# A recurrence on one core: one scan and one subtraction for both halves of the state, instead of two scans and a subtraction

## The chip, the cores and the metric

The kernel runs on one core of a Trainium2 chip. Its engines are TensorE (PE in the profile; its weight loads stand apart as PEld), VectorE (DVE), ScalarE (ACT), GpSimd (POOL) and SyncE (SP, which issues DMAs). They run side by side and wait for each other by semaphores. The metric is the device time of one execution in microseconds (us).

## The reference

Four graph layers follow each other on 1250 nodes with 512 features, each with a residual and a layer norm. The change touches only the recurrence in the first layer:

```
def gru(x_seq, W_ih, W_hh, b_ih, b_hh):
    pre_i = x_seq @ W_ih.T + b_ih            # 1250 x 1536
    def step(h, pi):
        ph = h @ W_hh.T + b_hh
        r = sigmoid(pi[:H] + ph[:H])
        z = sigmoid(pi[H:2*H] + ph[H:2*H])
        n = tanh(pi[2*H:] + r * ph[2*H:])
        h_new = (1.0 - z) * n + z * h
        return (h_new, h_new)
    _, ys = scan(step, zeros(H), pre_i)      # H = 512, 1250 steps, one after the other
```

## The kernel before

**Stages.** The edges are counted into dense adjacency matrices, two graph convolutions follow, then the input side of the recurrence (`pre_i`, kept in `big`), then the recurrence itself, then the other three layers. Each stage waits for the one before it, so a stage's time adds to the whole.

**The state.** The 512 elements of the state lie on 128 partitions as four blocks of 128. Two blocks form a half: c (of outputs) or kc (of inputs) is 0 or 1. The products are made in f16, with weights and state each split into a high and a low part. `h16` holds the state's parts. The weights' parts are in `whh16`: gates r and z (g = 0, 1) in memory that the profile names r, gate n (g = 2) in memory that it names hn. DVE holds the state scaled by HS = 4096.

**A product.** `gru_gate(u, c, kc, g)` issues, for gate g, the products of state half kc into output half c: two output blocks j by two input blocks k by two parts of the weights. One product is a 128x128 weight load and a matmul whose moving data is the state's one or two columns, repeated 16 times (COPIES). The low weights (part 1) meet the high state alone: 16 columns. The high weights (part 0) meet both: 32 columns. The results go to PSUM bank 4c + g, with the second output block at column offset 3 for gates r and z and at offset 4 for gate n. All low-weight products of a gate come before its high-weight products.

**Order on TensorE in a step.** Half 0 of the state into gates r, z, n of output half 0 (24 products), into r of half 1 (8) and half of n of half 1 (4); then half 1 of the state into r, z, n of half 0 (24), into r of half 1 (8); the other half of n (4), half 1 into n (8); last the z gate of half 1 (8 + 8). That is 96. Waits stand ahead of the first products that use the high part of a state half (`gru_state` 2t + 1), again ahead of the first that use its low part (2t + 2), and ahead of gates whose PSUM columns ScalarE fills with `pre_i` and bias (`gru_put0`, `gru_put1`).

**The rest of a step, for each half.** DVE adds the columns of r and of z with a scan of 6 elements (`scan_rz`, line 997); ScalarE takes the sigmoids (lines 719 and 724); DVE scans n's 8 columns with r as factor (`scan_n`, line 1003); ScalarE takes the tanh (line 728). Then DVE's `update` (line 1011) scans 8 elements, four per block, to the new state; `high_part` (line 1014) runs the same scan again with f16 output; `low_part` (line 1020) subtracts the high part from the f32 value. POOL (lines 328 and 329) prepares the next update's addends and keeps the state in `r1`. ScalarE's `put` (line 706) writes the next step's inputs into PSUM: three calls after the r sigmoid of half 1, two at the end. Each engine runs its instructions in the written order.

Of the kernel before, what the change touches and what calls it, by code (L numbers as in the profile page):

```python
# [25 lines left out]
ACT = mybir.ActivationFunctionType  # L26
# [8 lines left out]
P = 128  # L35
# [9 lines left out]
HS = 4096.0  # L45
XS = 2.0 ** 10
# [8 lines left out]
def layout(nc, io):  # L55

    ctx = ExitStack()
    with ctx:
# [99 lines left out]
        h16 = sb("h16", [P, 2, 2, 16], F16)  # L158
# [6 lines left out]
        upd_mul = sb("upd_mul", [P, 2, 8])  # L165
        upd_add = sb("upd_add", [P, 2, 8])
        upd = sb("upd", [P, 2, 2, 8])
# [35 lines left out]
        def _(sp):  # L203
# [44 lines left out]
            for c in range(2):  # L248
                sp.wait_ge(s(f"gru_put{c}"), (N + 1) * (1, 3)[c])
# [35 lines left out]
        def _(pool):  # L285
# [35 lines left out]
            with pool.Fori(0, N // 2) as i:  # L321
                for u in range(2):
                    t = 2 * i + u
                    for c in range(2):
                        pool.wait_ge(s(f"gru_state{c}"), 2 * t + 3)
                        pool.wait_ge(s(f"gru_upd{c}"), t + 1)
                        new, start = (a.rearrange("p (j a) -> p j a", a=4) for a in (upd[:, 1 - u, c], upd_add[:, c]))
                        pool.tensor_tensor(start[:, :, 1:3], new[:, :, 2:3].broadcast_to([P, 2, 2]), signs[:].rearrange("p (j a) -> p j a", a=2), ALU.mult).then_inc(s(f"gru_fresh{c}"), 1)  # L328
                        pool.tensor_copy(r1[:, 2 * c:2 * c + 2, bass.ds(t, 1)], upd[:, 1 - u, c, 2:8:4]).then_inc(s(f"gru_kept{c}"), 1)  # L329
# [20 lines left out]
        def _(pe):  # L350
# [141 lines left out]
            def gru_gate(u, c, kc, g, pieces=every, part=None):  # L492

                if part is None:
                    gru_gate(u, c, kc, g, pieces, 1)
                    return gru_gate(u, c, kc, g, pieces, 0)
                for j, k in pieces:
                    at = (4 if g == 2 else 3) * j
                    places = psum[:, 4 * c + g, 0:8 * COPIES].rearrange("p (r a) -> p r a", a=8)[:, :, at:at + 2 - part]
                    state = h16[:, u, kc, 8 * k + 6:8 * k + 8 - part]  # L500
                    m = mm(places, whh16[g][:, part, 2 * kc + k, (2 * c + j) * P:(2 * c + j + 1) * P],  # L501
                           state.unsqueeze(1).broadcast_to([P, COPIES, 2 - part]), start=(kc == 0 and j == 0 and k == 0 and part == 1),
                           stop=(kc == 1 and k == 1 and part == 0), skip_group_check=True)
# [769 lines left out]
```

## Time and profile before

| | |
|---|---|
| median of 3 runs | 5311.0 us (5308.29 to 5320.85) |
| the profiled execution | 5311.0 us, span 5308.3 us |
| the recurrence in the span | about 782 to 4172 us |
| busy over the span | PE 96%, PEld 81%, DVE 56%, ACT 41%, POOL 18% |
| mean granted TensorE clock | 0.961 of full speed |

The page lists groups of instructions by source line. Matmuls are pipelined: the profile shows each from its start to its modelled end, so they overlap, and how densely they are issued is seen in the starts or in the number of them in a stretch, not in the busy time. "Idle before" is an engine's idle time ahead of an instruction, with what ended it.

### The profile page before, as it was taken

What the parts mean: (1) busy time and instruction counts of PE and PEld (TensorE: products, weight loads), DVE (VectorE), ACT (ScalarE), POOL (GpSimd) and SP (SyncE); (2) the same over time, 40 slices, a digit from 0 to 9 for tenths busy, and PEclk for the clock granted to TensorE, in tenths of its full rate; (3) what the DMA queues carried; (4) which work ended last, traced back from release to release, by engine and by line L of the source; (5) the groups of instructions that cost most, each with busy time, mean ns of one, the idle gap of its engine ahead of it and who ended that gap; (6) DMA issues with size and microseconds to landing.
All of it is one profiled execution on the core that took longest, in us unless ns stands there. A gap on an engine that the chain in (4) does not pass through costs nothing.

```text
span 5308.3 us, 338777 instructions
## 1 busy us (share of the span) xinstructions
PE 5099.5 (96%) x128234; PEld 4274.3 (81%) x128235; DVE 2948.9 (56%) x16450; ACT 2160.5 (41%) x15422; POOL 948.7 (18%) x5221
## 2 busy tenths in 40 slices
PE   6669999999999999999999999999999999999989
PEld 4555559999999999999999999999999645555654
DVE  6662336666666666666666666666666444455551
ACT  0110005555555555555555555555555201221110
POOL 1230002222222222222222222222222100000000
PEclk7559999999999999999999999999999999999989
DMA  1002220000000000000000000000000100000011
GB/s 59 0 4 96 79 87 0 0 0 0 0 0 0 0 0 0 0 0 0 0 0 0 0 0 0 0 0 0 0 0 0 54 2 16 35 35 35 19 46 45
DMA packets 28930, 81.07 MB, mean 15 GB/s; under 512 B 1594, under 2 KB 1834, under 8 KB 28858
## 3 DMA queue, kind: packets, MB, share of 16 engines
q1 hardware_dynamic: 28858, 80.03, 4.1%
q8 instruction: 55, 0.90, 0.1%
q14 instruction: 17, 0.14, 0.0%
HBM read 58.08 MB, written 21.95 MB: 15 GB/s over the span
## 4 chain that ended last, share of the span: by engine, by line
PE 92%; DVE 3%; issue 2%; DVEq 2%; ACT 0%; POOL 0%; DMA 0%; SPq 0%; POOLq 0%; ACTq 0%
PE psum L501 64%; PE psum L570 8%; PE psum L376 5%; PE psum L366 4%; PE psum L582 4%; PE psum L483 2%; PE psum L556 2%; PE psum L646 1%; PE psum L423 1%; DVE r L879 1%; DVEq L874 1%; DVE r L878 1%; DVEq L872 1%; DVEq L871 1%; PE psum L433 0%
## 5 line engine op out<-in xcount | busy, mean ns | idle before, releaser
L501 PE MATMUL psum<-h,r 128*128 128x16 f16 (+1 forms) x80000 | 3087.7, 181 | 9.1 <-DVE h L1014 4.4
L501 PEld LDWEIGHTS psum<-h,r 128*128 128x128 f16 x80000 | 2555.9, 96 | 125.6 <-ACT psum L706 5.0
L501 PE MATMUL psum<-h,hn 128*128 128x16 f16 (+1 forms) x40000 | 1798.1, 177 | 0.0
L501 PEld LDWEIGHTS psum<-h,hn 128*128 128x128 f16 x40000 | 1416.7, 96 | 0.0
L997 DVE TENSOR_TENSOR_SCAN sum_rz<-mul_rz,psum 128x6 f32<-128x6 f32 x5000 | 814.6, 163 | 570.1 <-PE psum L501 511.5
L719 ACT ACTIVATE mul_n<-sum_rz 128x2 f32<-128x2 f32 x2500 | 517.7, 207 | 1198.9 <-DVE sum_rz L997 1198.9
L328 POOL TENSOR_TENSOR upd_add<-upd,signs 128x4 f32<-128x4 f32 x2500 | 500.5, 200 | 2731.3 <-DVE h L1014 1566.7
L706 ACT COPY psum<-big 128x2 f32 (+1 forms) x7506 | 931.0, 158 | 0.0
L1011 DVE TENSOR_TENSOR_SCAN upd<-upd_mul,upd_add 128x8 f32<-128x8 f32 x2500 | 437.0, 175 | 528.3 <-ACT upd_mul L724 373.0
L728 ACT ACTIVATE upd_add<-sum_n 128x2 f32<-128x2 f32 x2500 | 516.5, 207 | 271.5 <-DVE sum_n L1003 268.7
L724 ACT ACTIVATE upd_mul<-sum_rz 128x2 f32<-128x2 f32 x2500 | 493.7, 197 | 7.5
L1003 DVE TENSOR_TENSOR_SCAN sum_n<-mul_n,psum 128x8 f32<-128x8 f32 x2500 | 426.9, 171 | 122.2
L329 POOL COPY r<-upd 128x2 f32 x2500 | 470.8, 188 | 0.0
L1020 DVE TENSOR_TENSOR h<-upd,h 128x2 f16<-128x2 f32 x2500 | 421.9, 169 | 85.4
L1014 DVE TENSOR_TENSOR_SCAN h<-upd_mul,upd_add 128x8 f16<-128x8 f32 x2500 | 408.4, 163 | 0.0
L423 PE MATMUL psum<-r 125*128 125x100 bf16 x2580 | 238.3, 270 | 68.6 <-DVE r L879 62.0
L423 PEld LDWEIGHTS psum<-r 125*128 125x128 bf16 x2580 | 191.4, 132 | 109.8 <-DVE r L879 109.1
L376 PE MATMUL psum<-adj,hn 125*128 125x417 f32 (+1 forms) x720 | 252.7, 512 | 2.1 <-ACT hn L671 1.4
L376 PEld LDWEIGHTS psum<-adj,hn 125*128 125x128 f32 x720 | 135.7, 189 | 119.6 <-issue 115.0
L878 DVE TENSOR_SCALAR r<-r,hn 125x1254 bf16<-125x1254 f16 x258 | 151.7, 588 | 138.9 <-issue 101.1
L570 PE MATMUL psum<-adj,r 128*125 128x512 f16 x960 | 220.7, 388 | 8.3 <-DVE r L1199 8.3
L570 PEld LDWEIGHTS psum<-adj,r 128*125 128x125 f16 x960 | 133.5, 139 | 89.5 <-issue 16.2
(231 smaller groups left out, 2791.4 us busy)
## 6 DMA issues: line engine op xcount, KB each, us to landing
ws<-in_Wl SPq DMA_DIRECT2D x9, 1024.0 KB, 5.3
ws<-in_Wr SPq DMA_DIRECT2D x9, 1024.0 KB, 8.4
edge_counts<-adj SPq DMA_DIRECT2D x2, 3051.8 KB
edge_weights<-big SPq DMA_DIRECT2D x1, 6103.5 KB
adj_rows<-big SPq DMA_DIRECT2D x1, 6103.5 KB
adj<-adj_rows SPq DMA_DIRECT2D x1, 6103.5 KB
big<-edge_counts SPq DMA_DIRECT2D x1, 6103.5 KB
adj<-edge_weights SPq DMA_DIRECT2D x1, 6103.5 KB
```

The costliest lines, as they stand in the source:

```text
L328: pool.tensor_tensor(start[:, :, 1:3], new[:, :, 2:3].broadcast_to([P, 2, 2]), signs[:].rearrange("p (j a) -> p j a", a=2), ALU.mult).then ...
L329: pool.tensor_copy(r1[:, 2 * c:2 * c + 2, bass.ds(t, 1)], upd[:, 1 - u, c, 2:8:4]).then_inc(s(f"gru_kept{c}"), 1)
L376: m = mm(o[:, 0:n1 - n0], rows[0:NP, t, f * P:(f + 1) * P], mat[0:NP, t, n0:n1], start=(t == 0), stop=(t == NT - 1))
L423: m = mm(psum[:, 2 * u + t // 5, (t % 5) * 100:(t % 5) * 100 + 100], src_hot[0:EP, h, t * NP:t * NP + P], dst_hot[0:EP, h], start=False, s ...
L501: m = mm(places, whh16[g][:, part, 2 * kc + k, (2 * c + j) * P:(2 * c + j + 1) * P], state.unsqueeze(1).broadcast_to([P, COPIES, 2 - part] ...
L570: m = mm(o, a(pa), b(pb), start=start and i == 0, stop=stop and i == 2)
L706: return nc.scalar.copy(columns, big[:, bass.ds(t * 12 + c * 6 + 2 * g, 2)])
L719: nc.scalar.activation(mul_n[:, c, 3:8:4], sum_rz[:, c, 0, 2:6:3], ACT.Sigmoid).then_inc(s(f"gru_r{c}"), 1)
L724: nc.scalar.activation(upd_mul[:, c, 2:8:4], sum_rz[:, c, 1, 2:6:3], ACT.Sigmoid).then_inc(s(f"gru_z{c}"), 1)
L728: nc.scalar.activation(upd_add[:, c, 0:8:4], sum_n[:, c, 3:8:4], ACT.Tanh).then_inc(s(f"gru_n{c}"), 1)
L997: v.tensor_tensor_scan(sum_rz[:, c, g], mul_rz[:], psum[:, 4 * c + g, 0:6], 0.0, ALU.mult, ALU.add).then_inc(s(f"gru_{'rz'[g]}_sum{c}"), 1)
L1011: v.tensor_tensor_scan(upd[:, 1 - u, c], upd_mul[:, c], upd_add[:, c], 0.0, ALU.mult, ALU.add).then_inc(s(f"gru_upd{c}"), 1)
```

## The change

- The update scan becomes 14 elements, seven per block. After the new state and its multiple by 4096 it adds and takes away ROUND = 1.5 x 2^24, which leaves the value rounded to a coarse grid (the high part), and then a zero. The second scan is gone.
- One subtraction, `new_state`, yields for each block the pair (scaled state less high part, high part less zero), which is (low, high), in f16.
- There is one `gru_state` signal per half and step. TensorE no longer begins on the high part alone.
- Every product moves both columns: the low weights meet the low part too, 32 columns for all 96. The order within a gate goes over the parts innermost.
- ScalarE puts n's inputs of half 1 ahead of the z gate of half 1, and the signals are regrouped: `gru_put1` for r and n together, `gru_putz1` for z.
- POOL waits for the update scan alone. Strides of the update's arrays go from 4 to 7.

```
-            def gru_gate(u, c, kc, g, pieces=every, part=None):
-                if part is None:
-                    gru_gate(u, c, kc, g, pieces, 1)
-                    return gru_gate(u, c, kc, g, pieces, 0)
+            def gru_gate(u, c, kc, g, pieces=every):
                 for j, k in pieces:
                     at = (4 if g == 2 else 3) * j
-                    places = psum[:, 4 * c + g, 0:8 * COPIES].rearrange("p (r a) -> p r a", a=8)[:, :, at:at + 2 - part]
-                    state = h16[:, u, kc, 8 * k + 6:8 * k + 8 - part]
-                    m = mm(places, whh16[g][:, part, 2 * kc + k, (2 * c + j) * P:(2 * c + j + 1) * P],
-                           state.unsqueeze(1).broadcast_to([P, COPIES, 2 - part]), ...)
+                    for part in range(2):
+                        m = mm(psum[:, 4 * c + g, 0:8 * COPIES].rearrange("p (r a) -> p r a", a=8)[:, :, at:at + 2],
+                               whh16[g][:, part, 2 * kc + k, (2 * c + j) * P:(2 * c + j + 1) * P],
+                               h16[:, u, kc, k].unsqueeze(1).broadcast_to([P, COPIES, 2]), ...)
...
-                    pe.wait_ge(s("gru_state0"), 2 * t + 1)
+                    pe.wait_ge(s("gru_state0"), t + 1)
                     pe.wait_ge(s("gru_put0"), t + 1)
-                    gru_gate(u, 0, 0, 0, part=1)
-                    pe.wait_ge(s("gru_state0"), 2 * t + 2)
-                    gru_gate(u, 0, 0, 0, part=0)
-                    for g in (1, 2):
+                    for g in range(3):
                         gru_gate(u, 0, 0, g)
-                    pe.wait_ge(s("gru_put1"), 3 * t + 1)
+                    pe.wait_ge(s("gru_put1"), t + 1)
                     gru_gate(u, 1, 0, 0)
-                    pe.wait_ge(s("gru_put1"), 3 * t + 2)
                     gru_gate(u, 1, 0, 2, every[:2])
-                    pe.wait_ge(s("gru_state1"), 2 * t + 1)
-                    gru_gate(u, 0, 1, 0, part=1)
-                    pe.wait_ge(s("gru_state1"), 2 * t + 2)
-                    gru_gate(u, 0, 1, 0, part=0).then_inc(s("gru_r_mm0"), 1)
+                    pe.wait_ge(s("gru_state1"), t + 1)
+                    gru_gate(u, 0, 1, 0).then_inc(s("gru_r_mm0"), 1)
...
-                    pe.wait_ge(s("gru_put1"), 3 * t + 3)
+                    pe.wait_ge(s("gru_putz1"), t + 1)
...
-                    put(t + 1, 1, 0).then_inc(s("gru_put1"), 1)
+                    put(t + 1, 1, 0)
                     gate_n(1)
+                    put(t + 1, 1, 2).then_inc(s("gru_put1"), 1)
                     gate_z(1)
-                    put(t + 1, 1, 2).then_inc(s("gru_put1"), 1)
-                    put(t + 1, 1, 1).then_inc(s("gru_put1"), 1)
+                    put(t + 1, 1, 1).then_inc(s("gru_putz1"), 1)
...
-            def high_part(u, c):
-                v.tensor_tensor_scan(h16[:, 1 - u, c, 0:16:2], upd_mul[:, c], upd_add[:, c], 0.0, ALU.mult, ALU.add).then_inc(s(f"gru_state{c}"), 1)
-            def low_part(t, u, c):
-                dve.wait_ge(s(f"gru_state{c}"), 2 * t + 3)
+            def new_state(t, u, c):
                 dve.wait_ge(s(f"gru_upd{c}"), t + 1)
-                v.tensor_tensor(h16[:, 1 - u, c, 7:16:8], upd[:, 1 - u, c, 3:8:4], h16[:, 1 - u, c, 6:16:8], ALU.subtract).then_inc(s(f"gru_state{c}"), 1)
+                new = sevens(upd[:, 1 - u, c])
+                v.tensor_tensor(h16[:, 1 - u, c], new[:, :, 3:6:2], new[:, :, 5:7], ALU.subtract).then_inc(s(f"gru_state{c}"), 1)
```

## Rows read from the trace of the kernel before

**Rows 1.** The page: costliest groups and the chain that ended last, by line.
```profile
PE psum L501 64%; PE psum L570 8%; PE psum L376 5%; PE psum L366 4%; PE psum L582 4%; PE psum L483 2%; PE psum L556 2%; PE psum L646 1%; PE psum L423 1%; DVE r L879 1%; DVEq L874 1%; DVE r L878 1%; DVEq L872 1%; DVEq L871 1%; PE psum L433 0%
...
L501 PE MATMUL psum<-h,r 128*128 128x16 f16 (+1 forms) x80000 | 3087.7, 181 | 9.1 <-DVE h L1014 4.4
...
L501 PE MATMUL psum<-h,hn 128*128 128x16 f16 (+1 forms) x40000 | 1798.1, 177 | 0.0
```

**Rows 2.** Windows by stage: length, busy us (instructions) of PE, PEld, DVE, ACT, POOL; clock.
```profile
782.00:4172.00 3390.00, 3383.89 (x120000) 3267.90 (x120000) 2084.09 (x15000) 1911.81 (x15007) 808.51 (x4998) 1.00 0.00 0
```

**Rows 3.** Timeline over one step: start us, us, engine, line (DVE, ACT, POOL).
```profile
3000.24 0.17 DVE L1020 TENSOR_TENSOR h<-upd,h 128x2 f16<-128x2 f32 x1
...
3001.50 0.21 ACT L728 ACTIVATE upd_add<-sum_n 128x2 f32<-128x2 f32 x1
...
3001.74 0.17 DVE L1011 TENSOR_TENSOR_SCAN upd<-upd_mul,upd_add 128x8 f32<-128x8 f32 x1
3001.77 0.35 ACT L706 COPY psum<-big 128x2 f32 x3
3001.83 0.16 DVE L1014 TENSOR_TENSOR_SCAN h<-upd_mul,upd_add 128x8 f16<-128x8 f32 x1
3002.03 0.17 DVE L1020 TENSOR_TENSOR h<-upd,h 128x2 f16<-128x2 f32 x1
3002.13 0.17 DVE L1003 TENSOR_TENSOR_SCAN sum_n<-mul_n,psum 128x8 f32<-128x8 f32 x1
3002.16 0.20 POOL L328 TENSOR_TENSOR upd_add<-upd,signs 128x4 f32<-128x4 f32 x1 [1.55 <-DVE h L1014]
3002.21 0.15 DVE L997 TENSOR_TENSOR_SCAN sum_rz<-mul_rz,psum 128x6 f32<-128x6 f32 x1
...
3002.33 0.21 ACT L728 ACTIVATE upd_add<-sum_n 128x2 f32<-128x2 f32 x1 [0.21 <-DVE sum_n L1003]
3002.44 0.19 ACT L724 ACTIVATE upd_mul<-sum_rz 128x2 f32<-128x2 f32 x1
3002.54 0.24 ACT L706 COPY psum<-big 128x2 f32 x2
...
3002.66 0.17 DVE L1011 TENSOR_TENSOR_SCAN upd<-upd_mul,upd_add 128x8 f32<-128x8 f32 x1 [0.30 <-ACT upd_mul L724]
...
3004.44 0.17 DVE L1011 TENSOR_TENSOR_SCAN upd<-upd_mul,upd_add 128x8 f32<-128x8 f32 x1
```

**Rows 4.** The same timeline, TensorE's matmuls merged by tile.
```profile
3000.41 0.59 PE L501 MATMUL psum<-h,r 128*128 128x16 f16 x16
...
3002.79 0.38 PE L501 MATMUL psum<-h,r 128*128 128x16 f16 x8
...
3003.11 0.58 PE L501 MATMUL psum<-h,r 128*128 128x16 f16 x16
...
3003.53 0.36 PE L501 MATMUL psum<-h,hn 128*128 128x16 f16 x8
...
3003.95 0.46 PE L501 MATMUL psum<-h,hn 128*128 128x16 f16 x12
...
3004.26 1.20 PE L501 MATMUL psum<-h,r 128*128 128x16 f16 x32
```

**Rows 5.** Windows: weight loads (xN), then matmuls (xN) seen in growing stretches.
```profile
3002.03:3002.12 0.09, 0.00 (x0) 1.00 0.00 0
3002.03:3002.13 0.10, 0.01 (x1) 1.00 0.00 0
3002.03:3002.25 0.22, 0.13 (x4) 1.00 0.00 0
3002.03:3002.26 0.23, 0.14 (x5) 1.00 0.00 0
...
3001.90:3001.95 0.05, 0.05 (x9) 1.00 0.00 0
3001.90:3001.96 0.06, 0.06 (x10) 1.00 0.00 0
3001.90:3002.13 0.23, 0.23 (x10) 1.00 0.00 0
3001.90:3002.14 0.24, 0.24 (x11) 1.00 0.00 0
...
3002.15:3002.25 0.10, 0.10 (x4) 1.00 0.00 0
3002.15:3002.26 0.11, 0.11 (x5) 1.00 0.00 0
...
3002.15:3003.71 1.56, 1.56 (x59) 1.00 0.00 0
3002.15:3003.72 1.57, 1.57 (x60) 1.00 0.00 0
```

**Rows 6.** Views by line: durations in ns, min/median/max.
```profile
L997 DVE TENSOR_TENSOR_SCAN sum_rz<-mul_rz,psum x5000: 149/167/168, 784.3 to 4171.3; 128x6 f32<-128x6 f32 x193
...
L1003 DVE TENSOR_TENSOR_SCAN sum_n<-mul_n,psum x2500: 169/171/172, 784.8 to 4171.2; 128x8 f32<-128x8 f32 x193
...
L1011 DVE TENSOR_TENSOR_SCAN upd<-upd_mul,upd_add x2500: 173/175/191, 785.3 to 4171.8; 128x8 f32<-128x8 f32 x193
...
L1020 DVE TENSOR_TENSOR h<-upd,h x2500: 168/168/171, 785.5 to 4172.1; 128x2 f16<-128x2 f32 x193
```

**Rows 7.** Views by line of two kinds of sequencer instruction, same columns.
```profile
L510 PEldq ALU_OP  x1250: 32/34/36, 782.4 to 4168.4; - x179
...
L1002 DVEq EVENT_SEMAPHORE  x2500: 21/21/21, 784.7 to 4171.2; - x193
```

**Rows 8.** Groups by line and shape, 1000 to 4500 us: busy us, mean ns of one.
```profile
L501 PE MATMUL psum<-h,r 128*128 128x32 f16 x37496 | 2339.8, 184 | 0.0
L501 PE MATMUL psum<-h,r 128*128 128x16 f16 x37496 | 2297.0, 178 | 0.0
...
L501 PE MATMUL psum<-h,hn 128*128 128x32 f16 x18752 | 1301.3, 176 | 0.0
L501 PE MATMUL psum<-h,hn 128*128 128x16 f16 x18752 | 1273.5, 178 | 0.0
```

**Rows 9.** View of line 501, 1000 to 4000 us: ns min/median/max.
```profile
L501 PE MATMUL psum<-h,r x70944: 176/177/193, 1000.0 to 3999.8; 128*128 128x16 f16 x100, 128*128 128x32 f16 x100
...
L501 PE MATMUL psum<-h,hn x35481: 176/177/181, 999.8 to 4000.0; 128*128 128x16 f16 x100, 128*128 128x32 f16 x100
```

More of the change, by code:

```diff
@@ L45 @@
 HS = 4096.0
+ROUND = 1.5 * 2.0 ** 24
 XS = 2.0 ** 10
@@ L162, in layout @@
         sum_n = sb("sum_n", [P, 2, 8])
[L165 to L167 removed]
+        upd_mul = sb("upd_mul", [P, 2, 14])
+        upd_add = sb("upd_add", [P, 2, 14])
+        upd = sb("upd", [P, 2, 2, 14])
         signs = sb("signs", [P, 4])
@@ L324, in _ @@
                     for c in range(2):
-                        pool.wait_ge(s(f"gru_state{c}"), 2 * t + 3)
                         pool.wait_ge(s(f"gru_upd{c}"), t + 1)
-                        new, start = (a.rearrange("p (j a) -> p j a", a=4) for a in (upd[:, 1 - u, c], upd_add[:, c]))
+                        new, start = (a.rearrange("p (j a) -> p j a", a=7) for a in (upd[:, 1 - u, c], upd_add[:, c]))
                         pool.tensor_tensor(start[:, :, 1:3], new[:, :, 2:3].broadcast_to([P, 2, 2]), signs[:].rearrange("p (j a) -> p j a", a=2), ALU.mult).then_inc(s(f"gru_fresh{c}"), 1)
-                        pool.tensor_copy(r1[:, 2 * c:2 * c + 2, bass.ds(t, 1)], upd[:, 1 - u, c, 2:8:4]).then_inc(s(f"gru_kept{c}"), 1)
+                        pool.tensor_copy(r1[:, 2 * c:2 * c + 2, bass.ds(t, 1)], upd[:, 1 - u, c, 2:14:7]).then_inc(s(f"gru_kept{c}"), 1)
             def roots(n0, n1):
@@ L490, in _ @@
             every = ((0, 0), (0, 1), (1, 0), (1, 1))
-            def gru_gate(u, c, kc, g, pieces=every, part=None):
-                if part is None:
-                    gru_gate(u, c, kc, g, pieces, 1)
-                    return gru_gate(u, c, kc, g, pieces, 0)
+            def gru_gate(u, c, kc, g, pieces=every):
                 for j, k in pieces:
                     at = (4 if g == 2 else 3) * j
-                    places = psum[:, 4 * c + g, 0:8 * COPIES].rearrange("p (r a) -> p r a", a=8)[:, :, at:at + 2 - part]
-                    state = h16[:, u, kc, 8 * k + 6:8 * k + 8 - part]
-                    m = mm(places, whh16[g][:, part, 2 * kc + k, (2 * c + j) * P:(2 * c + j + 1) * P],
-                           state.unsqueeze(1).broadcast_to([P, COPIES, 2 - part]), start=(kc == 0 and j == 0 and k == 0 and part == 1),
-                           stop=(kc == 1 and k == 1 and part == 0), skip_group_check=True)
+                    for part in range(2):
+                        m = mm(psum[:, 4 * c + g, 0:8 * COPIES].rearrange("p (r a) -> p r a", a=8)[:, :, at:at + 2],
+                               whh16[g][:, part, 2 * kc + k, (2 * c + j) * P:(2 * c + j + 1) * P],
+                               h16[:, u, kc, k].unsqueeze(1).broadcast_to([P, COPIES, 2]), start=(kc == 0 and j == 0 and k == 0 and part == 0),
+                               stop=(kc == 1 and k == 1 and part == 1), skip_group_check=True)
                 return m
@@ L710, in _ @@
             put(0, 0, 2).then_inc(s("gru_put0"), 1)
-            for g in (0, 2, 1):
-                put(0, 1, g).then_inc(s("gru_put1"), 1)
+            put(0, 1, 0)
+            put(0, 1, 2).then_inc(s("gru_put1"), 1)
+            put(0, 1, 1).then_inc(s("gru_putz1"), 1)
             with act.Fori(0, N // 2) as i:
@@ L981, in _ @@
             link(v.memset(upd_mul[:], 1.0))
-            link(v.memset(upd_mul[:, :, 0:8:4], 0.0))
-            link(v.memset(upd_mul[:, :, 3:8:4], HS))
+            link(v.memset(upd_mul[:, :, 0:14:7], 0.0))
+            link(v.memset(upd_mul[:, :, 3:14:7], HS))
+            link(v.memset(upd_mul[:, :, 6:14:7], 0.0))
             link(v.memset(upd_add[:], 0.0))
+            link(v.memset(upd_add[:, :, 4:14:7], ROUND))
+            link(v.memset(upd_add[:, :, 5:14:7], -ROUND))
             link(v.memset(signs[:], 1.0))
@@ L991, in _, with sevens @@
             for c in range(2):
-                dve.sem_inc(s(f"gru_state{c}"), 2)
+                dve.sem_inc(s(f"gru_state{c}"), 1)
                 dve.sem_inc(s(f"gru_fresh{c}"), 1)
+            def sevens(ap):
+                return ap.rearrange("p (j a) -> p j a", a=7)
             def scan_rz(t, c, g):
```

18 lines of the change are left out of this document (9 added, 9 removed).

## The prediction

> **What bounds the kernel now.** I read the page first. The 1250 steps of the recurrence hold 120,000 of the 128,234 matmuls, and line 501 carries 64% of the chain that ended last [rows 1]. The windows by stage put the recurrence at 782 to 4172 us of the span, 3390 of 5308 us, with a granted clock of 1.00 [rows 2]: any change here is a number of nanoseconds per step, times 1250. "PE busy 100%" says nothing by itself, since one matmul is shown for some 177 ns and the next starts after some 26, so a pause shorter than that is invisible in the busy time. So I went to single steps.
>
> One step lasts from one update scan of column half 0 to the next, 3001.74 to 3004.44, 2.70 us [rows 3]. A step has 2 x 2 x 3 x 4 x 2 = 96 products (a weight load and a matmul each). The pieces of the TensorE timeline give their spacing: 16 products on the r tile in 3003.11 to 3003.53 (26.3 ns each), 12 on the hn tile in 3003.95 to 3004.26 (25.8 ns each) [rows 4]. At 26 ns, 96 products need 2.50 us, so 0.2 us per step is a pause. The windows that count products find it: the last of a step starts at 3001.96, the first of the next only at 3002.13; four have started by 3002.25, and only then does the fifth [rows 5]. That is the start of a step: product 1 waits for the high part of the new state (scan of line 1014, 3001.83 to 3002.00), product 5 for the low part (subtraction of line 1020, ends 3002.20) [rows 3].
>
> So the step is a loop of three stretches, and I use it for the sum. From the update scan's start to product 5: 3001.74 to 3002.26, 0.52 us. From product 5 to product 60, the last of the n gate of half 0 (24 + 8 + 4 + 24 = 60 products in issue order): 3002.26 to 3003.72, 1.46 us [rows 5]. From product 60 to the next update scan (matmul latency, scan, tanh): 3003.72 to 3004.44, 0.72 us [rows 3]. Together 2.70 us. TensorE's products 61 to 96 lie beside the third stretch and end before it does; that is the pause.
>
> Half 1 has a chain of its own. Its state is needed at product 37. Its low part ended at 3000.41, so product 41 could start at 3000.47; it started at about 3000.41 + 4 x 0.026 = 3000.51, in its turn [rows 3, 4]. It is near the bound, but it stops nothing: the spacing there stays 26 ns.
>
> **The change part by part.**
>
> *DVE.* The second scan (line 1014) goes. The update scan gets 14 elements instead of 8, and the subtraction that follows yields both f16 parts, 4 elements instead of 2. The 6-element scans take 167 ns and the 8-element ones 171 from PSUM: 2 ns an element [rows 6]; so the 14-element one takes 175 + 6 x 2 = 187 ns. The subtraction takes 168 for 2 elements [rows 6]; I add 2 to 4: 171. A dependent instruction starts some 30 to 40 ns after what it waits for (high part's end 3002.00, subtraction 3002.03; tanh's end 3001.71, update scan 3001.74) [rows 3]; I take 34. So both parts are there at 187 + 34 + 171 = 392 ns after the update scan's start. Before, the high part was there after 0.26 us (3001.74 to 3002.00) and the low part after 0.46. The complete state comes **64 ns sooner**, the high part alone 0.13 us later. If a scan element cost 1 or 4 ns, the 64 would be 70 or 52.
>
> *TensorE's wait.* Product 1 carries two waits, on the state and on the added-in inputs (gru_put0). Before, from the high part's end to its weight load were 3002.00 to 3002.12, some 0.12 us; product 5, with one wait, had its load at 3002.25 to 3002.26 after the low part's end at 3002.20, 0.05 to 0.06 us [rows 3, 5]. gru_put0 was no reason: ScalarE's three copies run from 3001.77 at 0.09 us spacing and the second, which is the one waited for, ends by 3002.03. The difference is a sequencer instruction between the two waits, the register operation of line 510, 34 ns long [rows 7]. In the changed code both waits compare with t + 1, so that operation should fall away, but the first wait still needs a carrier; on DVE a bare wait of this kind takes 21 ns [rows 7]. I take 0.12 - 0.013 = 0.11 us. So product 1's load now comes at 392 + 110 = 502 ns, its matmul 7 ns later: **0.51 us** after the update scan, where product 5 stood at 0.52. The bounds are 0.46 us (one wait's 0.057) and 0.52.
>
> *The early products.* Here is the price. Before, products 1 to 4 (low weights times the high part) were done when the low part came; now product 1 begins where product 5 began. **Four products more stand in the loop: 4 x 25.8 = 103 ns.**
>
> *Width.* The 48 products with the low weights now move 32 columns, not 16, and write both columns of a place. On width alone I add nothing: on the hn tile a 32-column matmul shows 176 ns and a 16-column one 178 [rows 8], and both kinds keep the spacing of 25.8. But on the r tile, where gates r and z are, the 32-column matmuls show 184 on average [rows 8]. Half of them (first output block, offset 0) should be like hn's 176, so the other half, whose pair of columns starts at offset 3, takes 192; the maximum of the r rows is 193, of the hn rows 181 [rows 9]. Offset 3 is odd, the n gate's second block starts at 4. The spacing shows a trace of it: 16 products with 4 such pairs took 0.42 us where 16 at hn's spacing would take 0.413 [rows 4], so 2 to 5 ns for each odd pair; I take 3.5. The change turns two odd pairs per r or z gate into four. The stretch from product 1 to 60 holds five such gates: **10 x 3.5 = 35 ns**. Bounds: 0 (the queue swallows it) and 10 x 16 = 160 ns (each shows its full 192 - 176). I stay near the spacing, as spacing is what the loop adds up.
>
> The Trainium skill bears on this: "PSUM — Partial Sum Buffer", Memory Cachelines, says PSUM has lines of two fp32 values and that every two consecutive elements should lie together for best throughput. A pair at offset 3 lies over two lines, and the trace agrees (192 against 176 ns). By that rule doubling the odd pairs is a real cost and the full 16 ns each, 160 per step, would be added if writing were the limit; by the spacing row it is 35. The rule speaks against the change in either case.
>
> *Reordered work.* ScalarE's copy into the n gate of half 1 is put ahead of the z gate of half 1, so that one semaphore covers r and n. It delays z's sigmoid, and so the second update scan, by one copy's spacing, 0.09 us. Behind it, DVE's queue is shorter by the removed scan (0.09 us) with 12 ns lost to the longer one, and the n scan of half 1, its tanh and the sigmoid come some 0.07 us sooner. Net: the second update scan moves from 0.92 us after the first (3002.66) to 0.94, its state is there at 0.94 + 0.39 = 1.33, usable at 1.39. Product 37 stood 0.98 us behind product 1 (3003.11 less 3002.13, a stop within), and comes now at 0.51 + 0.95 + 0.02 = 1.48 [rows 3 to 5]. No stall: worth nothing, with 0.09 us to spare. If the extra copy cost 0.19 us instead of 0.09, the cover would be gone. gru_put1 now comes after the tanh, near 3002.5 on the old clock, and product 25 needs it at 3002.79 [rows 4]; the queue behind that wait is all the rest of the step, but it is met. POOL starts up to 0.1 us sooner; it is idle 1.5 us before its pair of instructions and nobody waits for it. Its work, and removed sequencer work on all engines, lie off the loop: nothing. Set-up adds three small memsets, under 1 us.
>
> **Sum per step.** Update scan to product 1: 0.51. Product 1 to 60: 1.46 + 0.103 + 0.035 = 1.60. Product 60 to the next update: 0.72. Total 2.83 against 2.70. By differences: -64 (state) + 53 (two waits instead of one: 110 - 57) + 103 + 35 = **+127 ns**. Times 1250: +159 us. The profiled execution took 5311.0 us (span 5308.3 and 2.7 around it), which is also the median of the three, so 5311 + 159 = **5470 us**, 3.0% slower.
>
> **Rivals.**
> 1. *Slower, but less: the odd pairs cost nothing more and the wait is as short as product 5's.* For: the 7 ns of the spacing row are less than the view's rounding of 10. -35 alone gives +92 ns, 5426; with the short wait too (-53) +39 ns, 5360. 15%.
> 2. *Slower, and more: odd pairs in a row cost their shown 16 ns.* Four in sequence leave no room to catch up, which the trace of before, with two, never shows. +125 ns more: 5470 + 156 = 5626; half of it 5548. 15%. The skill's rule above is this rival at its full size.
> 3. *Faster: half 1 sets the step.* If the true setter were the state of half 1 (it ended at 3000.41 with its products right behind), then its chain's gain of 64 - 20 = 44 ns a step would be the result: 5311 - 55 = 5256. It decides if a pause stands before product 37. Against it: the pause of 0.17 us stands before product 1, and none before 37. 4%. From half 0's side a gain is out of reach: product 1 would have to start 0.13 us sooner than computed, at 0.38 us, and the subtraction ends at 0.39.
> 4. *No change.* The spacing of a stream of only 32-column products falls to 25 ns and the odd pairs vanish with the change of shape: 59 x 0.8 + 35 = 82 ns off, +45 ns; with the short wait (-53) it comes to -8 ns, 5301. It needs three lucky terms. 5%.
> 5. *The clock.* The pause grows from 0.17 to some 0.29 us per step. If the chip answered with 1.2 GHz instead of 2.4, all would be far slower. Against it: the granted clock is 1.00 over the recurrence with its pauses of 0.17 us [rows 2], and the columns moved rise by a third (2304 to 3072 a step). 1%.
>
> My forecast holds 60%, its own range 5430 to 5515.
>
> **Numbers.** 0.3% (16 us) is what a measurement of this kernel can tell from no change. Slower: 60 + 15 + 15 + 1 = 91%, less a little for rival 1's lower end: 90%. Same 6%, faster 4%. The range must leave out no more than 2 in 10: from 5370, within rival 1, to 5565, within rival 2.
>
> **What would show it.** The update scan at 185 to 190 ns and no second scan; the subtraction ending 0.39 us after its start; no products for 0.29 us at the start of a step, then no second stop after product 4; 16 products on the r tile in 0.43 to 0.44 us instead of 0.42; 32-column matmuls on r at 184 on average or a little more; a step of 2.83 us. I am wrong if product 1 starts less than 0.1 us after the state, if r products come 25 ns apart (both less), or if they come over 28 apart, or if a stop appears before product 37 (more).

## The result

The changed kernel takes 5340.93 us (median of 5 runs, 5339.82 to 5343.85), the kernel before 5309.69 us in the same comparison. The ratio is 1.0057, with a 95% interval of 1.0044 to 1.0072: slower by 31 us, clear of no change by a small margin. Forecast were 5470 us, with a range from 5370 to 5565. The sign was right and the size wrong by a factor of five, so the time lies below the range. In steps: 2.74 us instead of 2.70, where 2.83 was forecast.

The windows by stage put the excess where it was expected: the recurrence takes 3425 us (779 to 4204) instead of 3390, at a granted clock of 1.00 [rows 2]. The page of the changed kernel shows one new figure next to those of before [rows 1]: TensorE's idle time "before" rises from 9 to 44 us, since the pause at the start of a step (0.225 us from product 96 to product 1, 0.172 before) is now longer than the 193 ns that the step's last matmul is shown for.

```profile
L498 PE MATMUL psum<-h,r 128*128 128x32 f16 x80000 | 3109.0, 184 | 44.3 <-ACT psum L699 4.9
L498 PEld LDWEIGHTS psum<-h,r 128*128 128x128 f16 x80000 | 2539.7, 96 | 192.6 <-DVE h L1017 64.9
L498 PE MATMUL psum<-h,hn 128*128 128x32 f16 x40000 | 1776.1, 177 | 0.0
```

The timeline over one step of the changed kernel answers to [rows 3, 4]. Line 1011 is the update scan, line 1017 the one subtraction.

```profile
3001.40 0.19 DVE L1011 TENSOR_TENSOR_SCAN upd<-upd_mul,upd_add 128x14 f32<-128x14 f32 x1
3001.42 0.35 ACT L699 COPY psum<-big 128x2 f32 x3
3001.62 0.16 DVE L1017 TENSOR_TENSOR h<-upd 128x4 f16<-128x4 f32 x1
...
3002.28 0.35 PE L498 MATMUL psum<-h,hn 128*128 128x32 f16 x8
...
3002.33 0.19 DVE L1011 TENSOR_TENSOR_SCAN upd<-upd_mul,upd_add 128x14 f32<-128x14 f32 x1 [0.32 <-ACT upd_mul L718]
...
3002.80 0.59 PE L498 MATMUL psum<-h,r 128*128 128x32 f16 x16
...
3003.23 0.35 PE L498 MATMUL psum<-h,hn 128*128 128x32 f16 x8
...
3004.14 0.19 DVE L1011 TENSOR_TENSOR_SCAN upd<-upd_mul,upd_add 128x14 f32<-128x14 f32 x1
```

And the windows that count matmuls, as in [rows 5]: in those from 3001.55 the count stays at 10 from 3001.62 to 3001.83 and then product 1 comes; in those from 3001.86, where only product 1 and its followers are in sight, product 60 is the 60th, just before 3003.42.

```profile
3001.55:3001.61 0.06, 0.06 (x9) 1.00 0.00 0
3001.55:3001.62 0.07, 0.07 (x10) 1.00 0.00 0
3001.55:3001.83 0.28, 0.26 (x10) 1.00 0.00 0
3001.55:3001.84 0.29, 0.26 (x11) 1.00 0.00 0
3001.86:3003.40 1.54, 1.54 (x59) 1.00 0.00 0
3001.86:3003.41 1.55, 1.55 (x59) 1.00 0.00 0
3001.86:3003.42 1.56, 1.56 (x60) 1.00 0.00 0
```

So the subtraction ends at 3001.78, and product 1 starts at 3001.84, 0.06 us later. The forecast had 0.117. The loop's three stretches, in us; the measured ones are means over 1000 steps of each trace, from the starts of the same instructions:

| stretch | before | forecast | after |
|---|---|---|---|
| update scan to the full state's end | 0.457 | 0.392 | 0.384 |
| from there to the product that needs it | 0.063 (product 5) | 0.117 (product 1) | 0.057 (product 1) |
| that product to product 60 | 1.461 | 1.598 | 1.573 |
| product 60 to the next update scan | 0.725 | 0.72 | 0.725 |
| a step | 2.706 | 2.83 | 2.739 |

Two terms are off: the wait by 60 ns, the products by 25. The experiments take these, and the terms that came out right, one by one.

### The profile page after: what moved, and what is told of

Its sections match the earlier page's. It is cut to its first block, busy times and chain, and to the rows that moved or that the text cites. A ratio compares the mean times of both kernels' runs of the same rounds, so it can differ in the third digit from the quotient of the medians.

```text
span 5341.3 us, 325031 instructions
## 1 busy us (share of the span) xinstructions
PE 5093.8 (95%) x128234; PEld 4238.2 (79%) x128235; DVE 2851.6 (53%) x13953; ACT 2171.7 (41%) x15422; POOL 956.0 (18%) x5221
## 4 chain that ended last, share of the span: by engine, by line
issue 57%; PE 21%; POOL 13%; POOLq 3%; DVE 3%; DVEq 2%; ACT 0%; DMA 0%; SPq 0%; ACTq 0%
PE psum L563 8%; POOL upd_add L329 7%; POOL r L330 6%; PE psum L575 4%; PE psum L367 3%; POOLq L330 2%; PE psum L549 2%; PE psum L377 2%; PE psum L639 1%; PE psum L424 1%; DVE r L873 1%; DVEq L868 1%; POOLq L323 1%; DVE r L872 1%; DVEq L866 1%
## 5 line engine op out<-in xcount | busy, mean ns | idle before, releaser
L498 PE MATMUL psum<-h,r 128*128 128x32 f16 x80000 | 3109.0, 184 | 44.3 <-ACT psum L699 4.9
L498 PE MATMUL psum<-h,hn 128*128 128x32 f16 x40000 | 1776.1, 177 | 0.0
L498 PEld LDWEIGHTS psum<-h,hn 128*128 128x128 f16 x40000 | 1395.5, 96 | 0.0
L997 DVE TENSOR_TENSOR_SCAN sum_rz<-mul_rz,psum 128x6 f32<-128x6 f32 x5000 | 834.1, 167 | 693.0 <-PE psum L498 630.5
L699 ACT COPY psum<-big 128x2 f32 (+1 forms) x7506 | 1022.8, 158 | 0.0
L1011 DVE TENSOR_TENSOR_SCAN upd<-upd_mul,upd_add 128x14 f32<-128x14 f32 x2500 | 467.8, 187 | 544.7 <-ACT upd_mul L718 395.7
L718 ACT ACTIVATE upd_mul<-sum_rz 128x2 f32<-128x2 f32 x2500 | 508.2, 203 | 14.0 <-DVE sum_rz L997 0.2
L1017 DVE TENSOR_TENSOR h<-upd 128x4 f16<-128x4 f32 x2500 | 409.7, 164 | 86.0
L367 PE MATMUL psum<-ws,r 128*125 128x512 f32 x400 | 179.9, 612 | 7.2 <-ACT r L740 5.9
```

What stands on the lines that cost most here:

```text
L498: m = mm(psum[:, 4 * c + g, 0:8 * COPIES].rearrange("p (r a) -> p r a", a=8)[:, :, at:at + 2], whh16[g][:, part, 2 * kc + k, (2 * c + j) * ...
L699: return nc.scalar.copy(columns, big[:, bass.ds(t * 12 + c * 6 + 2 * g, 2)])
L718: nc.scalar.activation(upd_mul[:, c, 2:14:7], sum_rz[:, c, 1, 2:6:3], ACT.Sigmoid).then_inc(s(f"gru_z{c}"), 1)
L997: v.tensor_tensor_scan(sum_rz[:, c, g], mul_rz[:], psum[:, 4 * c + g, 0:6], 0.0, ALU.mult, ALU.add).then_inc(s(f"gru_{'rz'[g]}_sum{c}"), 1)
L1011: v.tensor_tensor_scan(upd[:, 1 - u, c], upd_mul[:, c], upd_add[:, c], 0.0, ALU.mult, ALU.add).then_inc(s(f"gru_upd{c}"), 1)
```

## The experiments

Times are medians; each ratio is to the kernel before, run on the same chip in turn, with its 95% interval. Steps and spacings given to the nanosecond are means over 1000 steps of the run's trace.

### Are the early products the price? (e3)

```
-                    pe.wait_ge(s("gru_state0"), 2 * t + 1)
                     pe.wait_ge(s("gru_put0"), t + 1)
-                    gru_gate(u, 0, 0, 0, part=1)
                     pe.wait_ge(s("gru_state0"), 2 * t + 2)
-                    gru_gate(u, 0, 0, 0, part=0)
-                    for g in (1, 2):
+                    for g in range(3):
                         gru_gate(u, 0, 0, g)
```

> The kernel before, but the first gate of a step no longer starts on the high part: TensorE waits for gru_put0 and the low part of half 0's state, and then issues all of gate r. Theory (products 1 to 4 done early are worth their issue time in the loop): product 1 starts where product 5 started, 0.52 us after the update scan, the step grows by 4 x 26 = 104 ns to 2.81 us, the time to about 5440. Rival (the restart of TensorE costs something each time it stops, so that one stop instead of two gives part back): 5400 to 5425. Rival (the early products were not in the loop): 5310.

Measured: 5437.41 us, ratio 1.0240 (1.0224 to 1.0257). The step is 2.807 us, 100 ns longer. The timeline shows it plainly (line 1017 is the subtraction here): the low part is ready at 3001.77, and the first weight load of the step, with all 60 products of the loop still to come, starts at 3001.82, after 0.22 us in which no weight load ran.

```profile
3001.31 0.17 DVE L1008 TENSOR_TENSOR_SCAN upd<-upd_mul,upd_add 128x8 f32<-128x8 f32 x1
3001.40 0.16 DVE L1011 TENSOR_TENSOR_SCAN h<-upd_mul,upd_add 128x8 f16<-128x8 f32 x1
3001.60 0.17 DVE L1017 TENSOR_TENSOR h<-upd,h 128x2 f16<-128x2 f32 x1
...
3001.82 0.48 PEld L501 LDWEIGHTS psum<-h,r 128*128 128x128 f16 x16 [0.22 <-DVE h L1017]
```

This part of the forecast (103 ns for four products) stands. It also says what the rest of the change is worth: the change gives up these 0.10 us and ends only 0.033 longer, so its other parts together gain 0.068 us.

### What does the wait at the start cost? (e1, e9)

e1 puts a register operation back between TensorE's two waits of the changed kernel.

```
                     pe.wait_ge(s("gru_state0"), t + 1)
-                    pe.wait_ge(s("gru_put0"), t + 1)
+                    pe.wait_ge(s("gru_put0"), 2 * t + 2)
...
-                    put(t + 1, 0, 2).then_inc(s("gru_put0"), 1)
+                    put(t + 1, 0, 2).then_inc(s("gru_put0"), 2)
```

The first signal, ahead of the loop, counts 2 as well; the waits behind the loop are changed to match.

> The changed kernel, but gru_put0 is counted in twos, so that TensorE's second wait at the start of a step compares with 2t + 2 and a register operation stands between the two waits, as before the change. Theory (my forecast overpriced the two waits: what cost 0.12 us in the kernel before was the register operation that carried the wait on the state, not the second wait): product 1 starts some 0.06 us later after the state than in the changed kernel (0.056 us from the subtraction's end to the first matmul there), the step grows from 2.739 to about 2.80 us, the time from 5341 to about 5417. Rival (the early signal of gru_put0 is what made it short, and the register operation runs ahead): no change, 5341.

Measured: 5434.80 us, ratio 1.0235 (1.0220 to 1.0251). Product 1 now starts 0.516 us after the update scan instead of 0.441, and the step is 2.811 us. In this trace the subtraction ends at 3002.73 (3002.57 + 0.16) and the first weight load of the step starts at 3002.86:

```profile
3002.57 0.16 DVE L1017 TENSOR_TENSOR h<-upd 128x4 f16<-128x4 f32 x1
...
3002.86 0.49 PEld L498 LDWEIGHTS psum<-h,r 128*128 128x128 f16 x16 [0.22 <-ACT psum L699]
```

0.13 us, where the changed kernel has 0.05 to its weight load. The effect is there and somewhat larger than expected: 75 ns at product 1, 72 a step. The view by line names the register operation:

```profile
L508 PEldq FUSED_REGOPS  x1250: 37/37/47, 784.1 to 4295.9; - x179
```

By the semaphores in the trace it is this operation that waits for the state; it starts 0.039 us after the subtraction's end, and the weight load of product 1, which now carries the wait on gru_put0, another 0.086 us later. With it the stretch is as forecast (0.516 against 0.51). So the forecast took the price of a sequencer operation that waits for the state and used it for a kernel in which nothing stands between that wait and the product. What stands at that line in the changed kernel is a bare wait, for gru_put0, which is early:

```profile
L508 PEldq EVENT_SEMAPHORE  x1250: 51/51/51, 779.3 to 4201.3; - x179
```

On average over 1000 steps it starts 0.314 us after the update scan and is over at 0.365; the state is complete at 0.384. So its 51 ns run while the state is still being made, if only with 0.02 us to spare, and the wait on the state itself is carried by the product's weight load.

e9 makes the same edit the other way round in the kernel before, so that both waits compare with 2t + 1 and need no register operation.

```
                     pe.wait_ge(s("gru_state0"), 2 * t + 1)
-                    pe.wait_ge(s("gru_put0"), t + 1)
+                    pe.wait_ge(s("gru_put0"), 2 * t + 1)
...
-                    put(t + 1, 0, 2).then_inc(s("gru_put0"), 1)
+                    put(t + 1, 0, 2).then_inc(s("gru_put0"), 2)
```

Here the first signal, ahead of the loop, stays at 1.

> The kernel before, but gru_put0 is counted in twos, so that both waits at the start of a step compare with 2t + 1 and no register operation stands between them. Theory (the 0.12 us from the high part to product 1 lay in the shadow of the low part, which product 5 waits for anyway): product 1 starts some 0.06 us sooner, 0.32 us after the update scan instead of 0.39, product 5 stays at 0.52, the step at 2.706 us and the time at 5310 within 8 us. Rival (the wait was in the loop before too, and the change profited from losing it): 0.03 to 0.06 us less per step, 5235 to 5270.

Measured: 5326.59 us, ratio 1.0038 (1.0024 to 1.0051), slower. Both expectations fell. Product 1 starts later, 0.421 us after the update scan (0.387 before), product 5 at 0.535 (0.520), and the step is 2.719 us. In the windows product 1 is the seventh in sight, at 3000.79, with the update scan at 3000.36; product 5 is at 3000.90.

```profile
3000.60:3000.78 0.18, 0.17 (x6) 1.00 0.00 0
3000.60:3000.79 0.19, 0.18 (x7) 1.00 0.00 0
3000.77:3000.89 0.12, 0.11 (x5) 1.00 0.00 0
3000.77:3000.90 0.13, 0.12 (x6) 1.00 0.00 0
```

The bare wait now is on gru_put0, and here that signal is the later of the two: the copy that gives it ends 0.276 us after the update scan, the high part 0.254.

```profile
L510 PEldq EVENT_SEMAPHORE  x1250: 51/51/51, 781.5 to 4183.6; - x179
```

From the end of that copy to product 1 are 0.145 us, of which the wait takes 51 ns. In these runs a signal that comes through a separate sequencer instruction costs 0.13 us (a register operation, kernel before and e1) to 0.145 (a bare wait, e9), one that the product carries 0.057. Which of two waits is carried is what matters, and it should be the later one. In the changed kernel it is, by 0.11 us.

### Do the odd pairs cost, and how much? (e2, e5)

e2 moves the second output block of gates r and z from column offset 3 to 4 in the changed kernel; the two scans over them get 8 elements. Not shown are the same strides in the arrays of these scans and in the sigmoids that read them.

```
-                    at = (4 if g == 2 else 3) * j
+                    at = 4 * j
...
-                columns = psum[:, 4 * c + 2, 3:8:4] if g == 2 else psum[:, 4 * c + g, 2:6:3]
+                columns = psum[:, 4 * c + 2, 3:8:4] if g == 2 else psum[:, 4 * c + g, 2:8:4]
...
-                v.tensor_tensor_scan(sum_rz[:, c, g], mul_rz[:], psum[:, 4 * c + g, 0:6], 0.0, ALU.mult, ALU.add)
+                v.tensor_tensor_scan(sum_rz[:, c, g], mul_rz[:], psum[:, 4 * c + g, 0:8], 0.0, ALU.mult, ALU.add)
```

> The changed kernel with the second output block of gates r and z at column offset 4 instead of 3 (places at 4j for all gates), and with scans of 8 instead of 6 elements for r and z. Theory (a pair of columns at an odd offset costs 4.2 ns of spacing, four per gate): all products come 25.0 ns apart, the five gates between product 1 and 60 save about 5 x 16.8 = 84 ns, which by half 0 gives a step of 2.655 us and 5236 us; but product 37 then comes 0.05 us sooner against a state of half 1 that had only some 0.03 us to spare, so a new stop of about 0.02 us before product 37 and about 5260. Rival A (the slower spacing belongs to the memory tile r of the weights, not to the offset): no change, 5341. Rival B (the longer scans of r and z are on the path): 4 ns of loss at most.

Measured: 5285.08 us, ratio 0.9951 (0.9937 to 0.9964), already faster than the kernel before. The groups by shape say why; first the changed kernel, then e2:

```profile
L498 PE MATMUL psum<-h,r 128*128 128x32 f16 x70110 | 2723.7, 184 | 34.6
```

```profile
L498 PE MATMUL psum<-h,r 128*128 128x32 f16 x71363 | 2624.9, 177 | 101.0
L498 PE MATMUL psum<-h,hn 128*128 128x32 f16 x35681 | 1567.9, 176 | 0.0
```

The slow matmuls on the r tile are gone (184 to 177 ns) while the weights' tile is the same, so it was the offset. In the starts, each of the four odd pairs of a gate in the changed kernel was followed by 29.2 ns instead of 25.0, all four alike; in e2 the spacing is 25.0. From product 1 to 36 that saves 50 ns, and the odd pairs behind it would save 33 more, but the step is only 48 ns shorter, because a new stop appears where it was expected, before product 37: half 1's state now comes last.

```profile
3001.46 0.17 DVE L1017 TENSOR_TENSOR h<-upd 128x4 f16<-128x4 f32 x1
...
3001.54 0.17 PEld L498 LDWEIGHTS psum<-h,hn 128*128 128x128 f16 x4
...
3001.68 0.47 PEld L498 LDWEIGHTS psum<-h,r 128*128 128x128 f16 x16
```

Four products at 25 ns take 0.10 us; the next weight load comes after 0.14, 0.05 after the subtraction's end at 3001.63. The stop costs 19 ns and the slower restart behind it 14, together 33 where 20 were expected; these 13 ns are 16 of the 25 us by which the time missed the expectation, and the other 9 stay open.

e5 makes the same edit in the kernel before.

> The kernel before with the second output block of gates r and z at column offset 4 instead of 3, and scans of 8 instead of 6 elements for r and z. Theory (an odd pair costs 4.2 to 5 ns of spacing, two per gate): products 5 to 60 lose about 9 ns in each of five gates, 46 ns, the step falls from 2.706 to 2.66 us and the time from 5310 to about 5253; half 1's low part, which had 0.03 us to spare before product 41, then stands close to it and may take 10 to 20 ns back, 5253 to 5275. Rival (the spacing belongs to the tile r): 5310.

Measured: 5263.13 us, ratio 0.9919 (0.9905 to 0.9932); the step is 2.670 us, 36 ns less, not 46. The two odd pairs per gate are gone from the spacing, and the 16-column products of r and z are spaced 26.3 to 26.7 ns instead of some 26, which takes part of it back.

### Is half 1 in the way? (e7, e8)

e7 puts ScalarE's copy for gate n of half 1 back behind the z gate in the changed kernel, e8 does so together with the even offset.

```
                     gate_n(1)
-                    put(t + 1, 1, 2).then_inc(s("gru_put1"), 1)
                     gate_z(1)
+                    put(t + 1, 1, 2).then_inc(s("gru_put1"), 1)
```

> The changed kernel with ScalarE's copy for gate n of half 1 back behind the z gate of half 1. Theory (half 1's state has about 0.03 us to spare before product 37, so its order of work does not matter): the second update scan comes some 0.09 us sooner or less, the time stays 5341 within 5 us. Rival (half 1 sets the step in part): up to 25 ns less, 5310.

Measured: 5344.49 us, ratio 1.0073 (1.0059 to 1.0086), as the changed kernel. The second update scan comes 0.886 us after the first instead of 0.931, and the step stays at 2.739 us.

> The changed kernel with both edits: column offset 4 for the second block of gates r and z, and the copy for gate n of half 1 back behind the z gate. Theory (once the odd pairs are gone, half 1's state sets part of the step, and the copy put in front of z is what makes it late): no stop before product 37, a step of 2.655 us, about 5236, some 20 us less than with the even offset alone. Rival (the even offset alone already has no such stop): the same time as with it alone.

Measured: 5232.60 us, ratio 0.9863 (0.9848 to 0.9878). This is the version that beats both: 77 us faster than the kernel before, 30 us faster than that kernel with even offsets (e5), and by the two ratios (1.0057 and 0.9863) some 100 us faster than the changed one. The step is 2.656 us, to a nanosecond what the three stretches give: 0.442 to product 1, 0.014 because product 2 follows it by 39 ns and not 25, 59 x 25.0 ns, and 0.725. The stop before product 37 is gone, and the second update scan comes 0.84 us after the first.

```profile
3000.72 0.19 DVE L1011 TENSOR_TENSOR_SCAN upd<-upd_mul,upd_add 128x14 f32<-128x14 f32 x1
...
3001.56 0.19 DVE L1011 TENSOR_TENSOR_SCAN upd<-upd_mul,upd_add 128x14 f32<-128x14 f32 x1 [0.28 <-ACT upd_mul L718]
...
3003.38 0.19 DVE L1011 TENSOR_TENSOR_SCAN upd<-upd_mul,upd_add 128x14 f32<-128x14 f32 x1
```

The same reordering is worth nothing in e7 and some 50 us here (0.9951 to 0.9863; some 20 were expected, as the stop that it removes had been priced too low): it only pays once the odd pairs no longer give half 1 its time.

### Why did wider products come closer together? (e4, e6, e11, e10)

From product 5 to 60 the changed kernel needs 1.458 us, the kernel before 1.461, although ten odd pairs were added. Something gave about 45 ns back. Some 12 of them are no gain: in the kernel before the stream restarts at product 5, inside this stretch (37.5 ns to product 6), in the changed one at product 1, ahead of it. The rest, some 32 ns, is closer spacing.

e6 goes back to an order with one part of the weights first and then the other (the high part first, where the kernel before had the low one first), all still at 32 columns:

```
-                for j, k in pieces:
-                    at = (4 if g == 2 else 3) * j
-                    for part in range(2):
+                for part in range(2):
+                    for j, k in pieces:
+                        at = (4 if g == 2 else 3) * j
```

> The changed kernel with the order within a gate as before: all products with the one part of the weights, then all with the other; every product still has 32 columns. Theory (width decides the spacing, not order): the same number of odd pairs, now in two groups of two per gate, each group of which costs 4.2 to 9 ns; the step is 2.739 us within 5 ns, 5341 within 8 us. Rival (two odd pairs in a row are partly absorbed, four are not): up to 20 ns less per step, 5316. Rival (alternating the parts is what makes the spacing 25.0): 0.8 ns more for each product, 47 ns, 5400.

Measured: 5342.06 us, ratio 1.0066 (1.0052 to 1.0080). No difference: this order decides nothing, and odd pairs in twos cost as much as in fours, 4.2 ns each.

e4 takes the width back: the low weights meet the high part alone. It leaves out the product of the two low parts, as the kernel before did.

```
-                        m = mm(psum[...][:, :, at:at + 2], ..., h16[:, u, kc, k].unsqueeze(1).broadcast_to([P, COPIES, 2]), ...)
+                        m = mm(psum[...][:, :, at + part:at + 2], ..., h16[:, u, kc, k, part:2].unsqueeze(1).broadcast_to([P, COPIES, 2 - part]), ...)
```

> The changed kernel, but the low weights meet the high part alone again (16 columns, single columns instead of pairs), in the changed kernel's order with the parts innermost. It leaves out the product of the two low parts, as the kernel before did. Theory (single columns are spaced 25.8 ns and pairs at an even offset 25.0, by width or contiguity; the odd pairs fall from four to two per gate): from product 1 to 60 the odd pairs give back about 40 ns and the 30 single-column products cost 30 x 0.8 = 24 ns, so the step is 2.72 us and the time about 5320. Rival (the 25.8 ns of before came from the order, low weights first): only the gain, 2.70 us, 5291.

Measured: 5338.12 us, ratio 1.0056 (1.0043 to 1.0069), no gain, and neither expectation. Half of the odd pairs are gone, which gives back 42 ns, but the stretch from product 1 to 60 is only 6 ns shorter: the starts in between are now up to 26.7 ns apart and not 25.0, and after an odd pair 29.9 or 30.1 instead of 29.2. That is 1.2 ns for each of the 30 single-column products. In the groups by shape the 16-column matmuls on the hn tile, where all pairs are even, are not shorter for their smaller width:

```profile
L498 PE MATMUL psum<-h,r 128*128 128x32 f16 x35126 | 2590.1, 184 | 47.2
L498 PE MATMUL psum<-h,r 128*128 128x16 f16 x35126 | 2539.3, 179 | 0.0
L498 PE MATMUL psum<-h,hn 128*128 128x16 f16 x17564 | 1454.9, 177 | 0.0
L498 PE MATMUL psum<-h,hn 128*128 128x32 f16 x17564 | 1450.5, 177 | 0.0
```

e11 asks what it is about 16 columns. It is e8 with the low weights on the high part alone, repeated 32 times: 32 single columns, eight places apart. It, too, leaves out the product of the two low parts.

```
+                        copies = (1 + part) * COPIES
-                        m = mm(psum[:, 4 * c + g, 0:8 * COPIES]...[:, :, at:at + 2], ...
+                        m = mm(psum[:, 4 * c + g, 0:8 * copies]...[:, :, at + part:at + 2], ...
```

> The changed kernel with even offsets and the copy for gate n put back (2.656 us a step, 5233 us), but the low weights meet the high part alone, repeated 32 times: 32 single columns, each eight places from the next, where that kernel writes 16 pairs. It leaves out the product of the two low parts, as the kernel before did. Theory A (each piece of PSUM that a matmul's columns touch costs, and 32 single columns touch as many as 16 odd pairs): such a matmul shows 189 to 193 ns and costs some 4.2 ns of spacing; product 1 to 60 takes 30 x 4.2 = 126 ns more, the step 2.78 us, the time about 5390. Theory B (only 32 columns as such matter, or only that a pair starts at an odd place): 176 ns, spacing 25.0 to 26 ns, 5233 to 5270.

Measured: 5474.21 us, ratio 1.0317 (1.0300 to 1.0335). With the same 32 columns per matmul as e8, the mean matmul goes from 176 ns to 184 and 185. First e8, then e11:

```profile
L498 PE MATMUL psum<-h,r 128*128 128x32 f16 x72308 | 2619.0, 176 | 102.2
```

```profile
L499 PE MATMUL psum<-h,r 128*128 128x32 f16 x67445 | 2686.1, 185 | 0.0
L499 PE MATMUL psum<-h,hn 128*128 128x32 f16 x33726 | 1627.4, 184 | 0.0
```

Single columns, 32 of them, cost at least what pairs over an odd place do, on both tiles. The spacing is 28.1 ns over all products, 3.1 more for each, not 4.2 for every second one as expected: from product 1 to 60 that is 178 ns and not 126. Besides, the stretch behind product 60 grew by 15 ns. So the step is 2.847 us, and the time missed Theory A's 5390 by 84 us. The 32 single columns also spread over twice as many places as the 16 pairs, and no run parts the two. "Advanced Engine Details and Errata", Memory Cachelines, of the Trainium skill (the prediction gives this section under another title) says that PSUM has lines of two fp32 values and that every two consecutive elements should be contiguous for best throughput. e2, e5, e4 and e11 agree: 4.2 ns for a pair over two lines, 1.2 for 16 single columns in e4, and 3.1 on average where half of the matmuls write 32 single columns.

e10 was to part 16 columns from single columns: e8 with COPIES = 8, so 16 columns in pairs. It computes the same state.

> The changed kernel with even offsets and the copy for gate n put back (2.656 us a step, 5233 us), with every product's columns repeated 8 times instead of 16, so 16 columns in pairs. It computes the same state, as the repeated columns are not read. Theory A (single columns, not 16 of them, made the spacing 25.8 to 26.7 ns): the spacing stays 25.0 ns and the time 5233 within 8 us. Theory B (16 columns as such give 25.8 ns or more): 59 x 0.8 to 1.2 ns more per step, 5290 to 5320. Rival to both (fewer columns moved bring the granted clock below 1.00 in the recurrence, as no kernel here has shown): hundreds of us more.

Measured: 5366.28 us, ratio 1.0111 (1.0095 to 1.0126). It answered another question, that of the rival in the expectation. The granted clock of the recurrence is 0.50, the 1.2 GHz level, from its start to its end:

```profile
779.00:4230.00 3451.00, 3411.26 (x119994) 3297.66 (x119991) 1992.66 (x12500) 1995.02 (x15000) 812.96 (x4999) 0.50 0.00 0
```

The rival's price, hundreds of us, was too high: the time is 134 us above e8. At that level the spacing is 26.7 ns, and nothing can be said about 16 columns in pairs at 2.4 GHz. That stays open. So 16 single columns are spaced wider than 32 in even pairs at the full clock, by 1.2 ns on average (e4), and whether their number or their being single does it is not settled.

## Why the prediction was wrong

**What bounds the kernel, and the loop.** Right. The three stretches add up to the measured step, and e3, e1 and e8 were computed from them to 3, 18 and 3 us. Where a price in them was unknown the miss was larger (e2 25, e11 84).

**DVE.** Right: update scan 187 ns (187 forecast), the state complete after 0.384 us (0.392); the subtraction took 164 ns, not 171.

**TensorE's wait.** This is the step that failed, in the forecast's words "the first wait still needs a carrier", taken as 0.11 us on the path. The carrier exists (51 ns, more than the 21 I took from DVE) but it holds the wait on gru_put0, whose signal comes 0.11 us before the state. Only the carried wait lies on the path: 57 ns to product 1, less than the 0.1 us that the prediction itself gave as a sign of being wrong. Price of the error: 60 ns a step, 75 us. I had this case as the lower bound and in rival 1. The trace showed that the operation of line 510 stood between the waits; I subtracted its length but kept it in the chain. e1 shows the forecast's stretch (0.516 us) when that operation is there.

**The early products.** Right: 103 ns forecast, 100 measured in e3.

**Width.** Half right. The odd pairs cost 10 x 4.2 = 42 ns with all the rest equal (35 forecast). "On width alone I add nothing" was wrong: with the low-weight products at 32 columns the spacing apart from odd pairs fell from as much as 26.7 ns to 25.0, some 32 ns less over product 5 to 60. The durations that I had, 178 ns for 16 columns and 176 for 32 [rows 8], pointed there; I read them as equal. Less the 7 ns that the odd pairs cost more than forecast, that is the 25 ns by which the products' term was too large.

**Reordered work.** Right that it stops nothing (e7), but with 0.03 us to spare, not 0.09, as the start of the step came sooner and the spacing was closer. e2 shows the stop once that is used up.

**Rivals.** The outcome lies below rival 1 (5360 to 5426): its short wait came true, its odd pairs at no cost did not. Of rival 4's three terms the closer spacing and the short wait came true and the vanishing of the odd pairs did not; by these two alone its sum would be 127 - 47 - 53 = 27 ns a step, near the 33 measured. Rival 2, 16 ns for each odd pair in a row, did not hold: four in a row cost 4.2 ns each. Rival 3, half 1 as setter, did not hold, and becomes true in e2. The clock stayed at 1.00; that all would be far slower at 1.2 GHz is contradicted by e10, with 2.760 us a step against 2.656.

In sum, the forecast's +127 ns a step were -64 for the state, +53 for the wait and +138 for the products. Measured are -73, -6 and +111, with 1 more in the last stretch: +33 ns. Times 1250 that is 41 us; the medians differ by 31 and the recurrence's own length by 35. The sign is a matter of layout and order as much as of the change's idea: with even places on both sides the change is still slower (e2 0.9951, e5 0.9919), with the copy of n put back as well it is faster (e8 0.9863).

## What to carry to other kernels

Where an instruction waits for two signals, find out which one it carries itself and which stands in a sequencer instruction ahead of it: here the first costs 0.057 us and the second 0.13 to 0.145 after its signal, so the later signal belongs on the instruction, and a price read from a pair of waits belongs to that arrangement only. Products that can start on part of the data were worth their whole issue time in this latency loop (four of them 0.10 us a step). Lay out PSUM columns so that pairs start at even places: that was worth 47 us in the kernel before and 56 in the changed one, and the next bound (here the second half's state) has to be moved with it to get the rest.

## What the runs showed of the hardware that was not expected

- A bare wait on TensorE's sequencer took 51 ns, on VectorE's 21 ns.
- A 128x128 f16 weight load and a matmul of 32 columns in even pairs are issued every 25.0 ns; in e4 each product with 16 single columns cost 1.2 ns more than that, so the narrower matmul is the slower.
- With the granted clock at 1.2 GHz for the whole recurrence (e10), the kernel lost only 2.5% against e8 (ratios 1.0111 and 0.9863): the pair of weight load and matmul took 26.7 ns instead of 25.0, which over 59 products is 98 of the 104 ns that the step grew, and the stretches before product 1 and behind product 60 stayed as they were (0.441 and 0.723 us). e10 differs from e8 in nothing but COPIES, 8 instead of 16, columns whose results no one reads; the two ran on different chips, but the kernel before kept a mean granted clock of 0.96 on the chip on which e10 had 0.64.
